# Layer norm scalings moved from ScalarE to VectorE, and two subtractions of the second layer's cut from GpSimd to VectorE

## The chip, the cores and the metric

The kernel runs on one core of one Trainium2 chip. The metric is the device time of one execution in microseconds (us), and lower is better. Five engines of the core work in parallel and meet at semaphores: TensorE (PE, with its weight loads PEld), VectorE (DVE), ScalarE (ACT), GpSimd (POOL) and SyncE (SP), which issues most of the DMAs.

## What is computed

Two layers on an x of 8 batches x 512 tokens x 128 channels, all in f32. Cut to what matters here:

```python
def _layernorm(x, axis=-1, eps=1e-05):
    m = jnp.mean(x, axis=axis, keepdims=True)
    v = jnp.var(x, axis=axis, keepdims=True)
    return (x - m) / jnp.sqrt(v + eps)
...
    x = L0_attn_x
    xn = _layernorm(x, axis=-1)
    x = x + _L0_attn_ref(xn, ...) + _L0_ffn_ref(xn, ...)
    xn = _layernorm(x, axis=-1)
    x = x + _L1_attn_ref(xn, ...) + _L1_ffn_ref(xn, ...)
    return x
```

Layer 0 is an attention over the 16 heads of one token, with a low-rank key and value projection and rotary angles, plus a gated feed-forward block. The attention of layer 1 is a Mamba mixer: it starts with an RMS norm of xn (so that xn is scaled a second time), makes a step dt, an input u and the vectors B and C for each token, and then runs the recurrence `h = exp(dt * A) * h + dt * B * u` over 512 tokens for 256 channels x 16 states, from which `y = sum(h * C)`. The feed-forward block of layer 1 is a mixture of 8 experts, two for each token, with one shared expert.

## The kernel before

**Tiling.** A batch is 512 tokens; a tile of tokens x channels is [128 partitions, TT = 4 groups of tokens, 128 channels], and turned by TensorE it is [128 channels, 512 tokens]. `layer0` handles the 8 batches in a software pipeline, one turn of its loop for a batch; `layer1` then does the recurrence batch by batch. Each engine has its own program, written out in the functions `gpsimd`, `scalar`, `vector` and `tensor`: the order of an engine's instructions is the order of its calls, and it waits in that order. Nothing is reordered when the kernel runs. A semaphore is wrapped in `Count`, so that `x.at(b, n)` is its value after the n-th step of batch b.

**Layer norm in layer 0.** Three engines make it. DVE takes the mean and variance (`statistics`, L767 to L775), POOL the power -0.5 (`root`, L518), DVE the product -mean * rstd (`shift_mean`, L780, tile `below`), and ACT applies it as `rstd * x + below`, one instruction of 128x128 for each of the four groups (`normalize`, L604, tile `xn`). PE then turns xn (`turn_x`, L1066), ACT copies it out of PSUM, and the projections follow (L1071 to L1087). The result of a batch is normalized again for layer 1: DVE's `pre_statistics` (L864 to L880), POOL's `second_root` (L539), DVE's `pre_means` (L884 to L888, tile `below2`), and ACT's `pre_normalize` with four instructions that write xn (L610; the tile `rows` lies in the memory that the profile calls `slots`) and four for the doubly normalized `xnr` (L616). PE turns both (L1184). The last batch is normalized so at the beginning of layer 1, in the calls of `tail`.

**Layer 1.** A batch has GROUPS = 32 steps, k = 0 to 31. In a step PE spreads one group of the input over the partitions (`spread_du`, L2098, into one of two PSUM banks `p_s_du`), DVE multiplies it by B (`inject`, L1980) and runs the recurrence (`scan`, L1988, tile `hs`), and ACT has made the decays three steps ahead (`decay`, L1881). After every second step POOL multiplies the two new tiles of hs by C (`times_c`, L1729), and after every fourth PE sums them (`gather_y`, L2112), standing in its queue ahead of the next `spread_du`. So POOL's pace reaches DVE through PE.

**Preparing the next batch.** In between, step by step, batch b + 1 is prepared while batch b is in the recurrence: softplus on ACT and DVE (L1959, L1964), `steps` on POOL (L1706, L1710, at k = 16 and 18), and the cut of dt * u into three bf16 parts whose sum is the f32 value. That cut is the chain that the change touches, for each of two halves s: ACT rounds the first part (`first_part`, L1856, k = 19 and 23); POOL subtracts it (`second_rest`, L1715, k = 20 and 24, tile `rest`, which shares memory with `conv`); ACT rounds the second part (`second_part`, L1860, k = 21 and 25); POOL subtracts again (`third_part`, L1720, k = 22 and 26). For batch 1 the same four subtractions are done by DVE, during layer 0 (L1969, L1974). The parts then go by DMA into the tile that PE spreads.

**What else stands in these queues.** POOL sends rows to the experts in batches 1 to 3 of layer 1 (L1747) and gathers the experts' sums in batches 4 to 8 (L1763), mostly at even steps; both are indirect DMAs that POOL issues. In batch 8, DVE takes five of the sixteen `times_c` (L1995). DVE also multiplies the experts' gate and up products (`half`, L2013), and ACT computes the gate's silu (L1896) after PE's down product of the unit before (L2171).

## Time and profile before

| | |
|---|---|
| median of 3 runs | 1091.25 us (1085.58 to 1091.52) |
| the profiled execution | 1085.58 us |
| its span in the trace | 1083.8 us, so 1.8 us lie around it |
| DVE busy | 869.2 us, 80% of the span |
| PE busy | 802.5 us, 74% |
| POOL busy | 632.8 us, 58% |
| ACT busy | 566.0 us, 52% |
| DMA engines | about 60% of the span |
| layer 0, until DVE's first scan | 446 us |
| layer 1 | the other 638 us, 74.6 to 78.5 us for a batch after the first |

An engine's busy share is an average over two layers with different limits. The first place to look is therefore the stage: busy time by engine in a stretch, then the waits in that stretch, then single instructions in order of time. "L1729" is line 1729 of the kernel before; an arrow `<-` in a wait names what ended it. Busy times of instructions that overlap at their ends are added up whole.

### The profile page before, as it was taken

How to read it: one execution, taken by the hardware profiler on the slowest of the kernel's cores; microseconds unless marked ns; L12 is line 12 of the kernel's file. 1: busy time of each engine (PE TensorE's matmuls, PEld its weight loads, DVE VectorE, ACT ScalarE, POOL GpSimd, SP SyncE). 2: the span in 40 equal slices, each digit the busy share in tenths (PEclk: the TensorE clock that was granted, in tenths of full speed). 3: DMA queues.
4: the chain of work that ended last, by engine and by line, in shares of the span. 5: the costliest groups of instructions: out<-in, count | busy, mean ns of one | idle time of the engine just before them, and what ended most of it. 6: DMA issues, size and time to landing. Idle time of an engine off the chain costs nothing. (4 is left out here: it accounts for less than half of the span.)

```text
span 1083.8 us, 12247 instructions
## 1 busy us (share of the span) xinstructions
PE 802.5 (74%) x3584; PEld 377.2 (35%) x3584; DVE 869.2 (80%) x1154; ACT 566.0 (52%) x888; POOL 632.8 (58%) x385
## 2 busy tenths in 40 slices
PE   3658778788797867488888789788888788743645
PEld 1112333333333323334544445344445444301211
DVE  2547878879778554689899899998898898995997
ACT  1122334333342353457787787786777776743420
POOL 1021121211221376337979979669989889689995
PEclk9659898898998897769999999899999999955665
DMA  4996568576562048451882873756957848626411
GB/s 131 220 196 164 152 147 224 160 175 195 146 160 83 15 119 219 117 153 40 240 240 80 212 226 97 190 153 159 241 140 180 200 115 192 157 48 137 82 20 35
DMA packets 85023, 161.48 MB, mean 149 GB/s; under 512 B 12603, under 2 KB 54748, under 8 KB 76636
## 3 DMA queue, kind: packets, MB, share of 16 engines
q1 hardware_dynamic: 73692, 152.26, 54.1%
q0 software_dynamic: 11264, 8.43, 4.6%
q8 instruction: 29, 0.48, 0.2%
q14 instruction: 38, 0.31, 0.1%
HBM read 116.26 MB, written 31.80 MB: 137 GB/s over the span
## 5 line engine op out<-in xcount | busy, mean ns | idle before, releaser
L1729 POOL TENSOR_TENSOR hs<-hs,c_rep 128x1024 f32<-128x1024 f32 x123 | 324.5, 2649 | 76.4 <-DVE hs L1988 75.6
L1980 DVE TENSOR_TENSOR p_s_du<-p_s_du,b_rep 128x512 f32<-128x512 f32 x256 | 174.4, 681 | 25.9 <-PE p_s_du L2098 25.5
L2098 PE MATMUL p_s_du<-block_in,spread 96*128 96x512 bf16 x256 | 110.2, 437 | 110.3 <-DVE hs L1988 110.0
L1988 DVE TENSOR_TENSOR_SCAN hs<-slots,p_s_du 128x512 f32<-128x512 f32 x108 | 131.8, 1221 | 10.8
L831 DVE TENSOR_TENSOR value_prod<-p_eb_y_acc,v 128x512 f32<-128x512 f32 x128 | 83.9, 685 | 39.4 <-PE p_eb_y_acc L1133 38.9
L1988 DVE TENSOR_TENSOR_SCAN hs<-steps,p_s_du 128x512 f32<-128x512 f32 x88 | 107.4, 1221 | 9.1 <-DVE p_s_du L1980 0.5
L1763 POOL DMA_INDIRECT y_xr<-moe_sums,position x64 | 103.0, 1610 | 11.6 <-issue 9.5
L522 POOL TENSOR_TENSOR sc<-ex,ex_part 128x1024 f32<-128x1024 f32 x8 | 17.0, 2128 | 157.5 <-ACT ex_part L647 157.5
L2112 PE MATMUL p_eb_y_acc<-hs,gather 128*32 128x512 f32 x512 | 81.1, 711 | 24.1 <-POOL hs L1729 19.4
L2098 PEld LDWEIGHTS p_s_du<-block_in,spread 96*128 96x128 bf16 x256 | 25.7, 101 | 202.7 <-DVE hs L1988 167.6
L807 DVE TENSOR_TENSOR score_prod<-qb,p_k_misc 128x2048 f32<-128x2048 f32 x32 | 72.4, 2283 | 13.0 <-issue 7.0
L1896 ACT ACTIVATE sg<-p_a_gu 128x1024 f32<-128x1024 f32 (+1 forms) x32 | 31.8, 994 | 59.1 <-PE p_acc_o L2171 47.9
L1881 ACT ACTIVATE steps<-steps,a_neg 128x512 f32<-128x512 f32 x88 | 60.1, 718 | 0.1
L539 POOL TENSOR_TENSOR root<-var,half 128x8 f32<-128x8 f32 x8 | 13.2, 1646 | 78.7 <-DVE var L880 78.7
L1988 DVE TENSOR_TENSOR_SCAN hs<-y_xr,p_s_du 128x512 f32<-128x512 f32 x44 | 53.7, 1221 | 4.7 <-DVE p_s_du L1980 0.5
L2070 PE MATMUL p_k_misc<-y_ht,wtap 128*128 128x512 f32 x112 | 56.9, 613 | 0.0
L2171 PEld LDWEIGHTS p_acc_o<-wm,sg 128*128 128x128 f32 x368 | 49.2, 198 | 17.4 <-issue 16.0
L2151 PE MATMUL p_a_gu<-xgt,wm 128*128 128x256 f32 x184 | 48.8, 388 | 3.3 <-ACT sg L1896 3.3
L2171 PE MATMUL p_acc_o<-wm,sg 128*128 128x128 f32 x368 | 51.1, 284 | 0.0
L1133 PE MATMUL p_eb_y_acc<-stack,over_d 96*128 96x512 bf16 x128 | 42.4, 390 | 10.8 <-DVE value_prod L831 9.9
L2140 PE MATMUL p_a_gu<-xgt,wm 128*128 128x256 f32 x184 | 49.2, 391 | 0.6 <-issue 0.4
L1881 ACT ACTIVATE slots<-slots,a_neg 128x512 f32<-128x512 f32 x60 | 40.9, 719 | 13.1 <-DVE hs L1988 13.0
(203 smaller groups left out, 1749.8 us busy)
## 6 DMA issues: line engine op xcount, KB each, us to landing
qb<-rq_rows SPq DMA_DIRECT2D x32, 1024.0 KB, 13.7
...
```

Source lines behind the costliest of these rows:

```text
L807: nc.vector.tensor_tensor(score_prod[:, i % 2], qb[:, i], p_k[:].unsqueeze(1).to_broadcast([128, 4, T]), ALU.mult)\
L831: nc.vector.tensor_tensor(value_prod[:, n % NP], p_eb[:, n % 2], v[:, b % NV], ALU.mult).then_inc(weighed.sem, 1)
L1729: nc.gpsimd.tensor_tensor(hs[:, n:n + 2], hs[:, n:n + 2], c, ALU.mult)\
L1763: nc.gpsimd.indirect_dma_start(xr[:, b - 1, t], None, moe["sums"][grp], bass.IndirectOffsetOnAxis(ap=position[:, grp, kk, TT * i + t:TT * ...
L1881: nc.scalar.activation(decay_of(b, k), steps_of[n % 3][:, bass.ts(j, T)], ACT.Exp, scale=a_neg[:, g:g + 1]).then_inc(da_done.sem, 1)
L1980: nc.vector.tensor_tensor(p_du[:, k % 2], p_du[:, k % 2], b_rep[p][:, order[k][3]], ALU.mult).then_inc(dbu_done.sem, 1)
L1988: nc.vector.tensor_tensor_scan(hs[:, n % NA], decay_of(b, k), p_du[:, k % 2], 0.0, ALU.mult, ALU.add).then_inc(scanned.sem, 1)
L2070: ins = nc.tensor.matmul(bank(b, U0 + n)[:, :], wtap[:, k, bass.ts(n, 128)], ht[:, b % 2, k:k + T], start=(k == 0), stop=(k == CONV - 1))
L2098: nc.tensor.matmul(p_du[:, k % 2], spread[:, i], block_in[:, (2 * b + s) % NB, j], start=True, stop=True).then_inc(du_full.sem, 1)
L2112: ins = nc.tensor.matmul(p_y[32 * j:32 * j + 32], w["gather"][:, i], hs[:, (GROUPS * (b - 1) + k) % NA], start=(i == 0 and h == 0), stop=( ...
L2140: ins = nc.tensor.matmul(p_gu[:, t, bass.ts(f, 256)], wm[:, (2 * j + t) % NR, bass.ts(f, 128)], xgt[:, j % 2, t], start=True, stop=True)
L2171: ins = nc.tensor.matmul(p_o[:, bass.ts(2 * t + i, 128)], sg[:, t, 256 * f + 128 * i:256 * f + 128 * i + 128], wm[:, (2 * j + t) % NR, 2 * ...
```

## The change

Two edits. The scaling of the layer norms becomes one DVE instruction for each group of 128x128, `(x - mean) * rstd` with both as values for each partition, and the products `below` and `below2`, their semaphores and their tiles go. And from batch 2 on the two subtractions of the cut are called in DVE's program at the same steps k, where they had been in POOL's.

```diff
@@ gpsimd of layer 0
         def root(b):
             pool.wait_ge(ln_var.sem, ln_var.at(b))
-            pool.wait_ge(ln_done.sem, ln_done.at(b - 1))
@@ residual
-            pool.wait_ge(pre_done.sem, pre_done.at(b, 1))
+            pool.wait_ge(pre_done.sem, pre_done.at(b, 2))
@@ scalar of layer 0
-        def normalize(b):
-            act.wait_ge(ln_shift.sem, ln_shift.at(b))
-            act.wait_ge(xt_full.sem, xt_full.at(b - 1))
-            for t in range(TT):
-                ins = nc.scalar.activation(xn[:, t], x[:, -b % NX, t], ACT.Identity, bias=below[:, t:t + 1], scale=rstd[:, t:t + 1])
-            ins.then_inc(ln_done.sem, 1)
...
@@ vector of layer 0
-        def shift_mean(b):
+        def normalize(b):
             dve.wait_ge(ln_rstd.sem, ln_rstd.at(b))
-            dve.wait_ge(ln_done.sem, ln_done.at(b - 1))
-            nc.vector.scalar_tensor_tensor(below[:], mv[:, :, 0], -1.0, rstd[:], ALU.mult, ALU.mult).then_inc(ln_shift.sem, 1)
+            dve.wait_ge(xt_full.sem, xt_full.at(b - 1))
+            for t in range(TT):
+                ins = nc.vector.tensor_scalar(xn[:, t], x[:, -b % NX, t], mv[:, t, 0:1], rstd[:, t:t + 1], ALU.subtract, ALU.mult)
+            ins.then_inc(ln_done.sem, 1)
...
-        def pre_means(b):
+        def pre_normalize(b):
             dve.wait_ge(pre_root.sem, pre_root.at(b))
-            nc.vector.tensor_tensor(rr[:], root2[:, 0], root2[:, 1], ALU.mult).then_inc(pre_shift.sem, 1)
-            dve.wait_ge(pre_done.sem, pre_done.at(b - 1))
-            nc.vector.scalar_tensor_tensor(below2[:, 0], mv2[:, :, 0], -1.0, root2[:, 0], ALU.mult, ALU.mult).then_inc(pre_shift.sem, 1)
-            dve.wait_ge(pre_shift.sem, pre_shift.at(b, 1))
-            nc.vector.scalar_tensor_tensor(below2[:, 1], mv2[:, :, 0], -1.0, rr[:], ALU.mult, ALU.mult).then_inc(pre_shift.sem, 1)
+            nc.vector.tensor_tensor(rr[:], root2[:, 0], root2[:, 1], ALU.mult).then_inc(pre_done.sem, 1)
+            for t in range(TT):
+                ins = nc.vector.tensor_scalar(rows[:, TT * (b - 1) + t, 0:D], x1[:, b % 2, t], mv2[:, t, 0:1], root2[:, 0, t:t + 1],
+                                              ALU.subtract, ALU.mult)
+            ins.then_inc(pre_done.sem, 1)
+            dve.wait_ge(pre_done.sem, pre_done.at(b, 1))
+            dve.wait_ge(pre_full.sem, pre_full.at(b - 1, 2))
+            for t in range(TT):
+                ins = nc.vector.tensor_scalar(xnr[:, t], x1[:, b % 2, t], mv2[:, t, 0:1], rr[:, t:t + 1], ALU.subtract, ALU.mult)
+            ins.then_inc(pre_done.sem, 1)
@@ gpsimd of layer 1, batch
-                if nxt and k in (20, 24):
-                    second_rest(b + 1, (k - 20) // 4)
-                if nxt and k in (22, 26):
-                    third_part(b + 1, (k - 22) // 4)
@@ vector of layer 1, batch
                 if k == 15:
                     softplus_end(b + 1)
+                if k in (20, 24):
+                    second_rest(b + 1, (k - 20) // 4)
+                if k in (22, 26):
+                    third_part(b + 1, (k - 22) // 4)
```

The lines of the changed kernel are numbered anew: `inject` is L1943 there, `scan` L1951, `half` L1976, the two subtractions L1932 and L1937, `times_c` of POOL L1696.

On DVE in layer 0, from the reciprocal of the softmax's denominators (tile `rden`) to the rotation of the queries (tile `turn`), before:

```order
L850 RECIPROCAL rden<-p_a_gu 128x512
L780 SCALAR_TENSOR_TENSOR below<-mv,rstd 128x4
L857 TENSOR_TENSOR x<-p_acc_o,x 128x512
L807 TENSOR_TENSOR score_prod<-qb,p_k_misc 128x2048
L864 BN_STATS stats<-x 128x6 x4
...
L807 TENSOR_TENSOR score_prod<-qb,p_k_misc 128x2048
L884 TENSOR_TENSOR rr<-root 128x4
L886 SCALAR_TENSOR_TENSOR below<-mv,root 128x4
L888 SCALAR_TENSOR_TENSOR below<-mv,rr 128x4
L785 SCALAR_TENSOR_TENSOR turn<-p_a_gu,bq,rope 128x512
```

and now:

```order
L822 RECIPROCAL rden<-p_a_gu 128x512
L751 TENSOR_SCALAR xn<-x,mv,rstd 128x128 x4
L829 TENSOR_TENSOR x<-p_acc_o,x 128x512
L779 TENSOR_TENSOR score_prod<-qb,p_k_misc 128x2048
L836 BN_STATS stats<-x 128x6 x4
...
L779 TENSOR_TENSOR score_prod<-qb,p_k_misc 128x2048
L856 TENSOR_TENSOR rr<-root 128x4
L858 TENSOR_SCALAR slots<-x,mv,root 128x128 x4
L864 TENSOR_SCALAR xnr<-x,mv,rr 128x128 x4
L757 SCALAR_TENSOR_TENSOR turn<-p_a_gu,bq,rope 128x512
```

Three instructions of 128x4 have become twelve of 128x128, and ACT no longer stands between `rstd` and PE.

On DVE in batch 1 of layer 1, from step k = 20 to k = 24, before:

```order
L1988 SCALAR_TENSOR_TENSOR hs<-slots,p_s_du 128x512
L2001 SCALAR_TENSOR_TENSOR yt<-u,vecs,p_eb_y_acc 128x512
L1980 TENSOR_TENSOR p_s_du<-p_s_du,b_rep 128x512
L1988 SCALAR_TENSOR_TENSOR hs<-slots,p_s_du 128x512
L1980 TENSOR_TENSOR p_s_du<-p_s_du,b_rep 128x512
L1988 SCALAR_TENSOR_TENSOR hs<-slots,p_s_du 128x512
L2013 SCALAR_TENSOR_TENSOR sg<-p_a_gu,sg 128x1024
L1980 TENSOR_TENSOR p_s_du<-p_s_du,b_rep 128x512
```

and now:

```order
L1951 SCALAR_TENSOR_TENSOR hs<-slots,p_s_du 128x512
L1964 SCALAR_TENSOR_TENSOR yt<-u,vecs,p_eb_y_acc 128x512
L1932 TENSOR_TENSOR conv<-dtu,y_part 128x512
L1943 TENSOR_TENSOR p_s_du<-p_s_du,b_rep 128x512
L1951 SCALAR_TENSOR_TENSOR hs<-slots,p_s_du 128x512
L1943 TENSOR_TENSOR p_s_du<-p_s_du,b_rep 128x512
L1951 SCALAR_TENSOR_TENSOR hs<-slots,p_s_du 128x512
L1976 SCALAR_TENSOR_TENSOR sg<-p_a_gu,sg 128x1024
L1937 TENSOR_TENSOR y_part<-conv,y_part 128x512
L1943 TENSOR_TENSOR p_s_du<-p_s_du,b_rep 128x512
```

A subtraction stands behind step 20 and another behind step 22, ahead of the next step's `inject`; two more follow behind steps 24 and 26.

On POOL in batch 3, from the second pair of `steps` (L1706, L1710) to the third `times_c` behind it, before:

```order
L1706 TENSOR_TENSOR dtu<-dtu 128x512
L1710 TENSOR_TENSOR dtu<-dtu,u 128x512
L1729 TENSOR_TENSOR hs<-hs,c_rep 128x1024
L1715 TENSOR_TENSOR conv<-dtu,y_part 128x512
L1736 TENSOR_TENSOR yt<-yt,sz 128x512
L1729 TENSOR_TENSOR hs<-hs,c_rep 128x1024
L1720 TENSOR_TENSOR y_part<-conv,y_part 128x512
L1729 TENSOR_TENSOR hs<-hs,c_rep 128x1024
```

and now:

```order
L1683 TENSOR_TENSOR dtu<-dtu 128x512
L1687 TENSOR_TENSOR dtu<-dtu,u 128x512
L1696 TENSOR_TENSOR hs<-hs,c_rep 128x1024
L1703 TENSOR_TENSOR yt<-yt,sz 128x512
L1696 TENSOR_TENSOR hs<-hs,c_rep 128x1024 x8
```

Of POOL's queue only the `times_c`, the gating of y (`yt`) and the indirect DMAs of other batches are left there.

## Rows read from the trace of the kernel before

**Rows 1.** The page, busy time, share of the span and instructions.

```profile
PE 802.5 (74%) x3584; PEld 377.2 (35%) x3584; DVE 869.2 (80%) x1154; ACT 566.0 (52%) x888; POOL 632.8 (58%) x385
```

**Rows 2.** Batches 3, 5, 7: us, busy PE PEld DVE ACT POOL, PEclk, DMA, GB/s.

```profile
613.00:687.00 74.00, 62.04 (x317) 35.13 (x310) 68.24 (x74) 58.85 (x92) 59.57 (x35) 1.00 0.66 174
763.00:841.00 78.00, 62.93 (x308) 35.81 (x300) 69.98 (x74) 59.24 (x92) 72.70 (x41) 0.98 0.74 186
919.00:996.00 77.00, 41.88 (x160) 15.06 (x156) 64.91 (x72) 43.65 (x66) 62.43 (x35) 0.68 0.50 113
```

**Rows 3.** Waits of DVE in layer 1, 446 to 1073 us.

```profile
DVE p_s_du L1980 <- PE p_s_du L2098: 25.5, 15, 5.8
DVE sg L2013 <- PE p_a_gu L2151: 7.4, 6, 2.0
```

**Rows 4.** Waits from 948 to 1005 us (end of batch 7): DVE, PE, POOL.

```profile
DVE p_s_du L1980 <- PE p_s_du L2098: 12.3, 3, 5.8
PE p_eb_y_acc L2112 <- POOL hs L1729: 13.9, 3, 6.2
POOL hs L1729 <- DVE hs L1988: 2.2, 2, 1.6
```

**Rows 5.** Groups by line: line, engine, out<-in | busy, mean ns | idle before.

```profile
L1729 POOL TENSOR_TENSOR hs<-hs,c_rep 128x1024 f32<-128x1024 f32 x123 | 324.5, 2649 | 76.4 <-DVE hs L1988 75.6
L1715 POOL TENSOR_TENSOR conv<-dtu,y_part 128x512 f32<-128x512 f32 x14 | 21.1, 1507 | 0.0
L1969 DVE TENSOR_TENSOR conv<-dtu,y_part 128x512 f32<-128x512 f32 x2 | 1.4, 688 | 9.4 <-ACT y_part L1856 9.4
```

**Rows 6.** Timeline of layer 0, a run of equal instructions on DVE: start, us.

```profile
227.16 2.48 DVE L831 TENSOR_TENSOR value_prod<-p_eb_y_acc,v 128x512 f32<-128x512 f32 x4
```

**Rows 7.** Timeline of batch 8: DVE's `times_c` beside POOL's work.

```profile
1044.36 2.95 POOL L1729 TENSOR_TENSOR hs<-hs,c_rep 128x1024 f32<-128x1024 f32 x1
1044.42 3.98 DVE L1995 TENSOR_TENSOR hs<-hs,c_rep 128x1024 f32<-128x1024 f32 x1
...
1059.55 1.56 POOL L1763 DMA_INDIRECT y_xr<-moe_sums,position  x1 [0.16 <-issue]
1060.57 1.23 DVE L1995 TENSOR_TENSOR hs<-hs,c_rep 128x1024 f32<-128x1024 f32 x1
```

**Rows 8.** Timeline of batch 2 around step k = 20.

```profile
587.29 1.02 ACT L1896 ACTIVATE sg<-p_a_gu 128x1024 f32<-128x1024 f32 x1 [3.08 <-PE p_acc_o L2171]
587.47 0.72 DVE L2001 SCALAR_TENSOR_TENSOR yt<-u,vecs,p_eb_y_acc 128x512 f32<-128x512 f32 x1
588.22 0.62 ACT L1856 ACTIVATE y_part<-dtu 128x512 bf16<-128x512 f32 x1
588.96 2.37 POOL L1729 TENSOR_TENSOR hs<-hs,c_rep 128x1024 f32<-128x1024 f32 x1
```

**Rows 9.** Waits of DVE around step 29, in batch 4, then in batch 2.

```profile
DVE sg L2013 <- PE p_a_gu L2151: 2.0, 1, 2.0
DVE p_s_du L1980 <- PE p_s_du L2098: 1.0, 1, 1.0
...
DVE sg L2013 <- PE p_a_gu L2151: 0.5, 1, 0.5
```

**Rows 10.** Timeline of layer 0, one turn of the loop.

```profile
248.21 1.65 ACT L604 ACTIVATE xn<-x,below,rstd 128x128 f32<-128x128 f32 x4 [10.64 <-DVE below L780]
249.91 0.66 PE L1066 MATMUL p_a_gu<-ident,xn 128*128 128x128 f32 x4 [2.79 <-ACT xn L604]
250.88 0.87 DVE L864 BATCH_NORM_STATS2 stats<-x 128x6 f32<-128x128 f32 x4
257.76 0.76 DVE L787 SCALAR_TENSOR_TENSOR p_a_gu<-p_a_gu,bq,rope 128x512 f32<-128x512 f32 x1 [0.69 <-PE p_a_gu L1077]
```

**Rows 11.** Timeline of the first steps of layer 1: PE, then DVE.

```profile
455.49 1.11 PE L1184 MATMUL p_acc_o<-ident,slots 128*128 128x128 f32 x4 [1.66 <-ACT slots L610]
462.08 0.70 DVE L1980 TENSOR_TENSOR p_s_du<-p_s_du,b_rep 128x512 f32<-128x512 f32 x1 [2.44 <-PE p_s_du L2098]
465.92 0.70 DVE L1980 TENSOR_TENSOR p_s_du<-p_s_du,b_rep 128x512 f32<-128x512 f32 x1 [1.82 <-PE p_s_du L2098]
```

47 lines of the change are left out of this document (9 added, 38 removed).

## Prediction

> **What bounds the kernel now.** I read the page first, then busy time by batch, then the waits of each layer, and last single instructions in order of time. The page has DVE as the busiest engine, with 80% of the span [rows 1]; but that is a mean over two layers. In layer 1, 446 us to the end, DVE is busy for 68.2 of 74 us in batch 3 and 70.0 of 78 in batch 5 [rows 2]. What it waits for there is short: 25.5 us for the next `p_s_du` of PE and 7.4 us for the experts' up product, of 627 us [rows 3]. So nearly everything put on DVE in layer 1 is put on the path.
>
> POOL is the second actor. In batch 5 it is busy for 72.7 of 78 us, in batch 3 only for 59.6 of 74 [rows 2]. It reaches DVE by way of PE, which stands at `gather_y` until POOL has multiplied, with DVE's next input queued behind. Where that happens is shown by the waits by stretch: 12.3 of the 25.5 us lie in the last third of batch 7 and the first steps of batch 8, where PE waits 13.9 us for POOL and POOL only 2.2 us for a scan [rows 4]. There POOL is the bound. In batches 4 to 6 POOL's lag costs DVE less: around step 29 of batch 4 it waits 2.0 and 1.0 us, in batch 2, with a shorter lag, 0.5 and nothing [rows 9]; 2.5 us for a batch. In batches 1 to 3 the DVE waits that are left follow PE's own queue.
>
> **Layer 1, the subtractions: DVE's own time.** Seven preparations (batches 2 to 8) with four subtractions each make 28 instructions more on DVE. One of this form takes 688 ns [rows 5]. In a row of equal ones the next starts before the last has ended: four take 2.48 us [rows 6], so the pitch is (2.48 - 0.69) / 3 = 0.60 us. That is 28 x 0.60 = 16.8 us, on the path.
>
> **What they wait for.** `second_rest` stands in DVE's queue right behind step 20, and the `inject` of step 21, with all of PE behind it, is queued behind it. It needs ACT's first part, and ACT makes that only after the silu at 587.29, which PE's down product has held up for 3.08 us. In batch 2 DVE is free about 588.1 (the 0.72 us from 587.47, less the overlap), and the first part is ready at 588.84 [rows 8]: 0.75 us of waiting. ACT's second silu of that kind, at step 25, does the same to the last subtraction at step 26. Both come before batches 2 to 7; in batch 7 there are no experts' products left and the wait isn't there. 6 x 1.5 = 9 us. Bounds: nothing, if PE and ACT run ahead once DVE is slower, and 14 us.
>
> **The port.** `conv<-dtu,y_part` has both inputs in SBUF; `inject` and `scan` have one in PSUM. Before shows what such an instruction of DVE does beside POOL: `times_c` on DVE takes 1.23 us when POOL is at an indirect DMA, but 3.98 us when POOL's `times_c` began 0.06 us ahead of it, and it ends 1.09 us after POOL's end (1048.40 against 1047.31) [rows 7]. So it stands still until POOL's instruction is over. The Trainium skill ("SBUF — State Buffer", Who interferes with whom) says that a DVE instruction with two SBUF inputs and a GpSimd instruction that reads SBUF exclude each other for a whole instruction, the first to start going first. By that rule each of the 28 instructions is exposed, and the trace agrees with it.
>
> The price of one meeting lies between 0 and 3.98 - 1.23 = 2.75 us [rows 7]. POOL's `times_c` takes 2.37 us early [rows 8] and 2.95 us late [rows 7]; sixteen of them are 38 us of batch 3's 74 and 47 us of batch 5's 78, 51 to 60% of the time, and more where POOL is late; with 65% in these steps a chance meeting costs half of one: 0.65 x 2.37 / 2 = 0.8 us early and 0.65 x 2.95 / 2 = 1.0 late, 3.2 and 4.0 us for four. Walking through batch 2 gives less, as the waits overlap: the first subtraction is ready at 588.9, in a tie with POOL's 588.96 [rows 8] (0 or 2.4 us); whichever wins, the second or third meets the next `times_c` for the rest of it. I get 2.6 us for the four in batches 1, 2 and 4 to 6, 0.7 in batch 3, where POOL is not late.
>
> **What comes back.** POOL loses four instructions of 1.5 us (1507 ns [rows 5]; about 1.2 us early and 1.75 late), 6 to 7 us for a batch. In batches 1 to 3 DVE didn't wait for that, so nothing comes back. In batches 4 to 6 the 2.5 us of a batch do [rows 9]. At the end of batch 7, where POOL is the bound, its 7 us are saved, and DVE's new work lies in waits that it had anyway; but POOL in its turn stands still while DVE's subtractions run, 4 x 0.6 = 2.4 us. I take -5.5 us; the bounds are 0 and all 12.3 us of [rows 4].
>
> Sum for layer 1, for each preparation, own time + ACT + port - returned: batches 1 and 2: 2.4 + 1.5 + 2.6 = 6.5 each; batch 3: 2.4 + 1.5 + 0.7 = 4.6; batches 4 to 6: 6.5 - 2.5 = 4.0 each; batch 7: -5.5. That is 13.0 + 4.6 + 12.0 - 5.5 = +24 us.
>
> **Layer 0.** DVE gets 12 instructions of 128x128 in a turn, and loses two small ones of 0.1 us and one that ran beside others. The trace has no such instruction in a row; the nearest is bn_stats of the same size, four in 0.87 us [rows 10], 0.2 us each. With two values for each partition I take the same 0.2: 2.4 us more, less 0.3, +2.1 in a turn; bounds 0.13 and 0.3 us each, 1.3 to 3.3 us in a turn. 
>
> What comes back in a turn: ACT's four take 1.65 us and PE waits 2.79 us for them [rows 10]. DVE has xn done about 1 us earlier; PE and the whole chain to the queries start that much sooner, and DVE's wait of 0.69 us for them [rows 10] goes; I count on another 0.6 us of its later waits for PE in the turn. That leaves about +0.8 us in each of six turns with a second normalization, nothing in the first two, where loads are waited for: +4 us (-4 to +12). At the start of layer 1, ACT's four for batch 8 hold PE up for 1.66 us, and DVE soon waits 2.44 and 1.82 us for PE [rows 11]. DVE pays 1.3 us more there and these waits shrink: -1.5 us (-3 to +1.3).
>
> **Sum.** 24 + 4 - 1.5 = +26.5 us on the profiled execution's 1085.6 (span 1083.8 and 1.8 around it): 1112.1 us. The median shown is 5.7 us above that execution. The changed kernel's median will lie likewise above, and I add half: 1115 us.
>
> **Rivals.**
> *The port costs nothing* and ACT is early. Then layer 1 is 16.8 - 7.5 - 7 = about +2, the whole +5: 1091 to 1097 us. For it: small DVE instructions beside POOL mostly don't stretch, and at steps 22 to 26 a slower DVE gives POOL time to finish. Against it: the 3.98 us, and that POOL is at work 75 to 93% of these batches [rows 2]. The port decides as soon as half of the 28 meet a `times_c`.
>
> *POOL is the bound from batch 4 on*, not only in batch 7. Then each of four batches gives back 7.0 - 2.4 = 4.6 us and DVE's additions are covered there: -18; batches 1 to 3 cost 3 x 2.4 = +7; and in layer 0 the shorter chain wins about 0.9 us in each of eight turns, -7. 1085.6 - 18 = 1068 us, faster. It decides if POOL has no idle time between a scan's end and its `times_c` over a whole batch. For it: 72.7 of 78 us in batch 5. Against it: 59.6 of 74 in batch 3, and DVE's few waits in batches 4 to 6.
>
> *Every subtraction meets a fresh `times_c`*, since POOL starts at the end of odd steps and the subtractions stand behind even ones, so that phases lock. 28 x (0.60 + 2.1) = 76 us, less 20 returned, +4: 1145 us.
>
> *The slower DVE starves PE* until its granted clock falls in batches 1 to 6, as it has in batch 7 (0.68 against 1.00 in batch 3 [rows 2]). PE's work would then show in DVE's waits: some us in each batch, and the time is 1125 to 1140 us.
>
> **Chances.** A measurement of this kernel tells about 1% from no change. My forecast's case, +12 to +40 us: 0.6. Port free: 0.2. POOL the bound: 0.1. The two dearer ones: 0.1 together. The low end of the range is that of the port-free case less a little for layer 0, 1088; the high end, 1137, leaves out the phase lock. Faster by over 1%: 0.09. Within 1%: 0.22, the port-free case and the low edge of mine. Slower by over 1% (above 1102): 0.69.
>
> **What would show it.** DVE's two subtraction lines at a mean well above 0.69 us, 1.2 to 1.6, with single ones near 3; POOL's instructions stretched by up to 0.6 us beside them; waits of DVE for ACT's parts near 0.75 us, twelve times; PE's waits for POOL in batches 4 to 8 mostly gone; batches 1 to 3 longer by 5 to 6 us, batch 7 shorter; a turn of layer 0 longer by under 1 us. If the subtractions average 0.7 us, the port step is wrong; if batches 4 to 6 are shorter than before, POOL was their bound; if layer 0 changes by more than 10 us, my pitch for the small ones is.

## The result, and the profile after

| | before | changed |
|---|---|---|
| median, us | 1091.38 (1085.58 to 1091.58) | 1140.57 (1135.68 to 1142.24) |
| profiled execution, span, us | 1083.8 | 1138.9 |
| first scan of layer 1 at, us | 445.85 | 470.75 |
| first scan to the end of the last, us | 627.4 | 657.6 |

The changed kernel is slower: ratio 1.0443, 95% interval 1.039 to 1.0498. The prediction said slower, at 1115 us; the result is 26 us above that and 3.6 us above the range. Of the profile's 55 us, 25 lie in layer 0, where 4 were forecast, and 30 in layer 1, where 24 were.

The page, as in [rows 1]:

```profile
PE 834.1 (73%) x3584; PEld 391.6 (34%) x3584; DVE 940.7 (83%) x1254; ACT 528.1 (46%) x792; POOL 605.2 (53%) x357
```

DVE is busy for 71.5 us more, with 100 more instructions. The 28 subtractions of layer 1 at 0.69 us would be 19 of these and the change in layer 0 some 22 (8 turns of 2.75, below); 30 us are not accounted for by such work. Batches 3, 5 and 7 of the changed kernel, as in [rows 2]:

```profile
652.00:729.00 77.00, 61.99 (x315) 35.32 (x311) 72.35 (x79) 59.08 (x92) 52.75 (x29) 1.00 0.60 158
810.00:894.00 84.00, 65.86 (x322) 37.27 (x321) 77.52 (x80) 59.29 (x92) 66.21 (x35) 0.96 0.66 169
976.00:1053.00 77.00, 42.44 (x153) 14.17 (x155) 72.67 (x76) 43.75 (x66) 61.14 (x32) 0.66 0.52 114
```

The granted clock in layer 1 is nearly what it was (1.00, 0.96, 0.66 against 1.00, 0.98, 0.68), so the starved-PE rival isn't at work there. POOL is busy for 7, 6 and 1 us less, and DVE for 4, 8 and 8 us more.

The waits of DVE in layer 1, which answer to [rows 3], and from 1020 us the waits for POOL, which answer to [rows 4]:

```profile
DVE conv L1932 <- ACT y_part L1819: 4.5, 6, 1.5
DVE p_s_du L1943 <- PE p_s_du L2065: 4.0, 4, 1.8
...
DVE y_part L1937 <- ACT y_part L1823: 1.9, 1, 1.9
...
PE p_eb_y_acc L2079 <- POOL hs L1696: 4.2, 4, 1.4
```

DVE's 25.5 us of waiting for the next product shrank to 4.0, and PE's wait for POOL at the end of batch 7 from 13.9 to 4.2: the relief of POOL is real. The two subtraction lines of DVE swallowed it. Groups by line, mean in ns:

```profile
L1932 DVE TENSOR_TENSOR conv<-dtu,y_part 128x512 f32<-128x512 f32 x16 | 33.2, 2075 | 11.7 <-ACT y_part L1819 11.7
L1937 DVE TENSOR_TENSOR y_part<-conv,y_part 128x512 bf16<-128x512 f32 x16 | 19.6, 1226 | 1.9 <-ACT y_part L1823 1.9
```

The timeline of batch 2 behind step 20, POOL and DVE together, and then that of batch 5:

```profile
620.44 4.45 DVE L1932 TENSOR_TENSOR conv<-dtu,y_part 128x512 f32<-128x512 f32 x1 [1.46 <-ACT y_part L1819]
620.75 2.36 POOL L1696 TENSOR_TENSOR hs<-hs,c_rep 128x1024 f32<-128x1024 f32 x1
623.06 1.27 POOL L1703 TENSOR_TENSOR yt<-yt,sz 128x512 f32<-128x512 f32 x1
...
860.95 5.37 DVE L1932 TENSOR_TENSOR conv<-dtu,y_part 128x512 f32<-128x512 f32 x1 [0.68 <-ACT y_part L1819]
861.59 2.96 POOL L1696 TENSOR_TENSOR hs<-hs,c_rep 128x1024 f32<-128x1024 f32 x1
863.90 1.86 POOL L1703 TENSOR_TENSOR yt<-yt,sz 128x512 f32<-128x512 f32 x1
```

Read the ends. POOL's second instruction ends at 624.33, DVE's subtraction at 624.89; at 865.76 and 866.32 in batch 5. DVE waited through two instructions of POOL in a row and ended 0.56 us behind the second, though it had begun 0.31 and 0.64 us before the first. 21 of the 28 subtractions meet POOL in this way, and all 21 end 0.55 to 0.56 us after POOL does. The 28 take 50.1 us; alone they would take 28 x 0.69 = 19.3. So the port costs DVE 30.8 us, in a layer that grew by 30.2. POOL's `times_c` are not stretched in return: they take 2.51 us in the mean, before 2.65.

The trace of before had such meetings already. DVE's first softplus instruction (L1959, two operands in SBUF, 1.22 us alone), in batch 2:

```profile
570.01 3.80 DVE L1959 SCALAR_TENSOR_TENSOR dtu<-conv,dtu 128x1024 f32<-128x1024 f32 x1
570.33 2.39 POOL L1729 TENSOR_TENSOR hs<-hs,c_rep 128x1024 f32<-128x1024 f32 x1
```

It began 0.32 us ahead of POOL's product and ended 1.09 us behind it. The other six of layer 1 met POOL too and took 1.32 to 3.09 us.

In layer 0 I take a turn from one `RECIPROCAL rden` of DVE to the next. Turn 3 before, then turns 3 and 4 after (busy PE, PEld, DVE, ACT, POOL, then PEclk):

```profile
156.52:200.61 44.09, 36.10 (x178) 14.78 (x178) 35.92 (x61) 16.54 (x28) 9.29 (x6) 0.92 0.68 180
```

```profile
161.31:207.41 46.10, 38.12 (x178) 15.53 (x178) 38.74 (x71) 11.71 (x16) 9.28 (x6) 0.89 0.67 172
207.41:257.86 50.45, 40.12 (x178) 16.68 (x178) 39.97 (x72) 11.71 (x16) 9.30 (x6) 0.86 0.61 157
```

DVE is busy 2.8 us longer in a turn (turn 4 has 1.2 us of setup for layer 1 in it, before as well). In turn 3 the rest of the turn, in which DVE isn't busy, is 7.4 us, in turn 4 10.5; before it was 8.2. The same turn 4 in stretches of 4 us:

```profile
220.00:224.00 4.00, 1.02 (x9) 0.71 (x6) 4.00 (x11) 1.09 (x2) 0.00 (x0) 1.00 0.31 68
224.00:228.00 4.00, 3.73 (x8) 1.18 (x7) 3.97 (x4) 0.00 (x0) 0.00 (x0) 0.65 0.17 66
228.00:232.00 4.00, 4.00 (x18) 2.21 (x18) 3.97 (x6) 2.08 (x3) 0.00 (x0) 0.50 0.77 197
232.00:236.00 4.00, 4.00 (x11) 0.61 (x12) 0.57 (x1) 0.30 (x2) 0.00 (x0) 0.50 1.01 217
236.00:240.00 4.00, 4.00 (x20) 2.18 (x18) 3.54 (x6) 0.87 (x2) 0.00 (x0) 0.65 1.04 229
```

PE had 1.02 us of work in 220 to 224 us; then its granted clock fell to 0.50, that is to 1.2 of 2.4 GHz, just as it had work without a gap, and from 232 to 236 us it was DVE that had next to nothing to do (0.57 of 4 us). What PE stood still for is in the timeline:

```profile
219.65 1.10 DVE L858 TENSOR_SCALAR slots<-x,mv,root 128x128 f32<-128x128 f32 x4
220.67 1.10 DVE L864 TENSOR_SCALAR xnr<-x,mv,rr 128x128 f32<-128x128 f32 x4
...
223.71 1.12 PE L1058 MATMUL p_a_gu<-lat,wup 33*128 33x512 f32 x2 [2.25 <-DVE turn L757]
...
236.29 1.29 DVE L803 TENSOR_TENSOR value_prod<-p_eb_y_acc,v 128x512 f32<-128x512 f32 x2 [3.72 <-PE p_eb_y_acc L1110]
```

The rotation of the queries (L757) had to stand behind the eight scalings and the setup. Four scalings start 1.02 us before the next four, 0.255 us each.

So three questions: is the port the whole of layer 1's loss; how much of layer 0's is DVE's own work and how much the clock; and do the two halves add up?

### The profile page after: what moved, and what is told of

It reads as the page before. It is cut to its first block and busy times, and to the rows that moved or that the text cites. A ratio compares the mean times of both kernels' runs of the same rounds, so it can differ in the third digit from the quotient of the medians.

```text
span 1138.9 us, 12206 instructions
## 1 busy us (share of the span) xinstructions
PE 834.1 (73%) x3584; PEld 391.6 (34%) x3584; DVE 940.7 (83%) x1254; ACT 528.1 (46%) x792; POOL 605.2 (53%) x357
## 5 line engine op out<-in xcount | busy, mean ns | idle before, releaser
L1696 POOL TENSOR_TENSOR hs<-hs,c_rep 128x1024 f32<-128x1024 f32 x123 | 309.3, 2514 | 131.3 <-DVE hs L1951 130.9
L2065 PE MATMUL p_s_du<-block_in,spread 96*128 96x512 bf16 x256 | 112.5, 442 | 165.4 <-DVE hs L1951 165.0
L1943 DVE TENSOR_TENSOR p_s_du<-p_s_du,b_rep 128x512 f32<-128x512 f32 x256 | 174.0, 680 | 4.2 <-PE p_s_du L2065 4.0
L1951 DVE TENSOR_TENSOR_SCAN hs<-slots,p_s_du 128x512 f32<-128x512 f32 x108 | 131.8, 1220 | 11.1 <-DVE p_s_du L1943 0.5
L1951 DVE TENSOR_TENSOR_SCAN hs<-steps,p_s_du 128x512 f32<-128x512 f32 x88 | 107.4, 1220 | 9.1 <-issue 0.4
L1730 POOL DMA_INDIRECT y_xr<-moe_sums,position x64 | 106.3, 1661 | 11.5 <-issue 8.2
L2037 PE MATMUL p_k_misc<-y_ht,wtap 128*128 128x512 f32 x112 | 60.3, 645 | 0.0
L534 POOL TENSOR_TENSOR root<-var,half 128x8 f32<-128x8 f32 x8 | 13.2, 1646 | 83.9 <-DVE var L852 83.9
L1951 DVE TENSOR_TENSOR_SCAN hs<-y_xr,p_s_du 128x512 f32<-128x512 f32 x44 | 53.7, 1220 | 4.7 <-DVE p_s_du L1943 0.5
L1074 PE MATMUL p_s_du<-score_prod,sum_d 128*32 128x512 f32 x256 | 48.0, 832 | 13.0 <-DVE score_prod L779 13.0
L2118 PE MATMUL p_a_gu<-xgt,wm 128*128 128x256 f32 x184 | 51.4, 404 | 1.9 <-ACT sg L1859 1.9
L1110 PE MATMUL p_eb_y_acc<-stack,over_d 96*128 96x512 bf16 x128 | 45.1, 413 | 9.2 <-DVE value_prod L803 7.3
L2107 PE MATMUL p_a_gu<-xgt,wm 128*128 128x256 f32 x184 | 50.5, 398 | 0.0
```

The costliest lines, as they stand in the source:

```text
L1696: nc.gpsimd.tensor_tensor(hs[:, n:n + 2], hs[:, n:n + 2], c, ALU.mult)\
L1730: nc.gpsimd.indirect_dma_start(xr[:, b - 1, t], None, moe["sums"][grp], bass.IndirectOffsetOnAxis(ap=position[:, grp, kk, TT * i + t:TT * ...
L1943: nc.vector.tensor_tensor(p_du[:, k % 2], p_du[:, k % 2], b_rep[p][:, order[k][3]], ALU.mult).then_inc(dbu_done.sem, 1)
L1951: nc.vector.tensor_tensor_scan(hs[:, n % NA], decay_of(b, k), p_du[:, k % 2], 0.0, ALU.mult, ALU.add).then_inc(scanned.sem, 1)
L2037: ins = nc.tensor.matmul(bank(b, U0 + n)[:, :], wtap[:, k, bass.ts(n, 128)], ht[:, b % 2, k:k + T], start=(k == 0), stop=(k == CONV - 1))
L2065: nc.tensor.matmul(p_du[:, k % 2], spread[:, i], block_in[:, (2 * b + s) % NB, j], start=True, stop=True).then_inc(du_full.sem, 1)
```

## The experiments

The kernel before was run beside each group: its median was 1095.5 us in the first, 1094.6 in the second and third, 1094.1 in the fourth.

### Each half alone

`e1_layer0_only` has the changed kernel's layer 0 and the subtractions on POOL; `e2_layer1_only` has the reverse.

```diff
 # e1, vector: batch()
-                if k in (20, 24):
-                    second_rest(b + 1, (k - 20) // 4)
-                if k in (22, 26):
-                    third_part(b + 1, (k - 22) // 4)
 # e1, gpsimd: batch()
+                if nxt and k in (20, 24):
+                    second_rest(b + 1, (k - 20) // 4)
+                if nxt and k in (22, 26):
+                    third_part(b + 1, (k - 22) // 4)
```

Expected of e1: 

> The layer norm edit alone: the scalings on DVE, the subtractions back on POOL. The two traces put DVE's first scan at 446 us before and 471 us after, so theory A (the two edits add up, and layer 0 alone has lost about 25 us, six times what I forecast) gives 1091 + 25 = 1116 us, with the first scan at 470 to 472. Theory B (layer 0 costs the 4 us of my sum and the rest of the 25 was brought about by something else, so that the edits don't add) gives 1095 us.

Expected of e2: 

> The subtractions alone on DVE, the scalings back on ACT. Theory A: layer 1 is 30 us longer as in the changed kernel, batch by batch +7, +8, +2, +6, +5, +4, 0, and the first scan stands at 446 us: 1121 us. My forecast for layer 1 by itself was +24, 1115 us. Theory B: the subtractions cost only DVE's own 17 us less what POOL's relief gives back: under 1105 us.

Measured: e1 1108.69 us, ratio 1.0113 (1.0064 to 1.0162); e2 1121.36 us, ratio 1.0226 (1.0167 to 1.0285). Both halves lose. e1 lies between its two forecasts: layer 0's part costs 13 us in the medians, not the 25 by which the two profiles differ. e2 is where theory A had it. The sum of the two, 3.4%, is under the first measurement of both together (4.4%) and near the second (3.9%, below). In e2 the 28 subtractions take 50.6 us, one by one nearly the durations of the changed kernel, with layer 0 untouched.

### Layer 0 in doses

`e3_norm_only` moves only the first normalization to DVE (4 scalings in a turn), `e4_pre_only` only the second (8). In both the subtractions stay on POOL.

```diff
 # e3, vector: main()
-            shift_mean(1)
+            normalize(1)
 # e4, vector: main()
-                    pre_means(b - 2)
+                    pre_normalize(b - 2)
```

Expected of e3: 

> Of the layer norm edit only the first normalization (four scalings of a batch, tile xn) on DVE; the second stays on ACT with its small products. It shortens the chain to PE by about 0.6 us and costs DVE 4 x 0.25 us less 0.1. Theory C (DVE's time costs what it is): between -2 and +6 us over eight batches, 1089 to 1097. Theory D (what costs is TensorE's clock, which falls after PE has been kept waiting, so that anything that feeds PE sooner is a gain): -5 to 0 us.

Expected of e4: 

> Only the second normalization (eight scalings of a batch) on DVE, the first on ACT as before. Theory D: this is the part that keeps PE waiting 2.3 us for the rotated queries and shifts the stretch at granted clock 0.5 into PE's fullest 12 us; nearly all of the 25 us is here: 1110 to 1116 us. Theory C (DVE's time alone): 8 x 0.25 = 2.0 us in a turn, 6 turns and the tail: +10 to +14 us, 1101 to 1105.

Measured: e3 1100.46 us, ratio 1.0022 (0.9978 to 1.0066); e4 1102.5 us, ratio 1.0078 (1.0042 to 1.0114). The first normalization alone costs nothing that can be told, though its median lies above both forecasts. The second alone costs what theory C gave it, far under theory D's; its 0.8% can't be told from the 1.1% of all twelve scalings.

### The scalings elsewhere, fewer of them, and once more

`e5_scalings_later` is the changed kernel with the four scalings into `xnr` behind `rope_q`; `k1_one_scaling` makes one instruction of each four, with the mean and factor of the first group for all four, so it leaves out the normalization of the other three; `a2_after_again` is the changed kernel itself.

```diff
 # e5, vector: main()
                 if b < B:
                     rope_q(b + 1)
+                if pre and new:
+                    pre_normalize_late(b - 2)
 # k1, in the three places
-            for t in range(TT):
-                ins = nc.vector.tensor_scalar(xn[:, t], x[:, -b % NX, t], mv[:, t, 0:1], rstd[:, t:t + 1], ...)
+            ins = nc.vector.tensor_scalar(xn[:], x[:, -b % NX], mv[:, 0, 0:1], rstd[:, 0:1], ...)
```

Expected of e5: 

> The changed kernel with one thing moved: the four scalings into xnr stand behind the three instructions that rotate the next batch's queries, not ahead of them (for the last but one batch they stay where they were). VectorE has the same work. If layer 0's loss is VectorE's own added time, nothing changes: 1139 to 1143 us, ratio 1.044, a first scan near 470 us. If it comes from TensorE waiting for the rotated queries and then working through the rest of the turn at a granted clock of 0.50, that wait (2.25 us) shrinks by about the 1.1 us of the four scalings, fewer turns have such a stretch, and the first scan comes at 455 to 462 us, the kernel at 1124 to 1132, ratio 1.030 to 1.036.

Expected of a2: 

> The changed kernel once more, for a second look at its layer 0. If the length of a turn goes by where TensorE's granted clock falls to 0.50 in it, the turns differ from the first profile's (48.8, 46.1, 50.5, 48.4, 46.9 us) or agree with them exactly as their low stretches do; the time is 1135 to 1143 us, ratio 1.040 to 1.049. If VectorE's own work set the turns, they would be as long in the run with layer 0's part alone (45.3, 45.3, 49.6, 45.2, 44.1), which they were not.

Expected of k1: 

> The changed kernel with each group of four 128x128 scalings of layer 0 as one instruction of 128x512, which takes the mean and factor of the first tile for all four, so the normalization of the other three tiles is left out. A group of four took 1.10 us; one of 128x512 should take 0.3 to 0.7 us. If VectorE's own added work is layer 0's loss, 1.2 to 2.4 us go from each turn: first scan 452 to 459 us instead of 466 to 471, ratio 1.026 to 1.032. If the loss is the granted clock or a wait, the turns keep their lengths: ratio 1.037 to 1.045.

Measured: e5 1136.87 us, ratio 1.0417 (1.0349 to 1.0485); a2 1137.7 us, ratio 1.039 (1.0317 to 1.0464); k1 1125.83 us, ratio 1.0277 (1.0216 to 1.0339). e5 moved four of the eight scalings ahead of the rotation out of PE's way; its time lies between its two forecasts, nearer to that of no change, and can't be told from a2's; its first scan comes at 465.4 us. a2's turns 2 to 6 (46.2, 48.2, 50.5, 45.2, 44.0 us) are not those of the first profile of the same kernel (48.8, 46.1, 50.5, 48.4, 46.8). Cutting their time did: in k1 one scaling of 128x512 takes 0.54 us where four of 128x128 took 1.10, and the kernel is 12 us faster than a2.

### TensorE's gaps filled

Two useless products on PE ahead of the turn of x in six turns, in the kernel before (`f1_before_filled`); the same and two more ahead of `project_k` in the changed kernel (`f2_after_filled`).

```diff
 # tensor: turn_x(b), for b > 2
+                for _ in range(2):
+                    nc.tensor.matmul(p_a0[:], wq[:, 0], xt[:, (b - 2) % NT], start=True, stop=True)
 # f2 also, main(): ahead of project_k(b + 1)
+                    for _ in range(2):
+                        nc.tensor.matmul(p_s[:, 1], wq[:, 0], xt[:, b % NT], start=True, stop=True)
```

Expected of f1: 

> The kernel before with two useless products (a 128x128 weight by 128x512, f32, 1.05 us each, written where the turn of x follows and overwrites them) on TensorE in six turns of layer 0, in the gap of 2.8 us in which it waits for the normalized x. All other engines have the same work. Clock theory: it is the thin work at the start of a turn after which the granted clock falls to 0.50 for some 6 to 8 us; with the gap filled it falls in fewer turns, a turn goes from 44.0 us toward the 41.1 us of the one turn seen without a low stretch, and the first scan comes at 432 to 443 us instead of 446 to 452; kernel 1077 to 1088, ratio 0.985 to 0.995. Rival, that the low stretch is covered by VectorE's work and costs nothing, or that two products change nothing about it: 1.000 within 0.4%, first scan 446 to 452.

Expected of f2: 

> The changed kernel with the same two products in the gap ahead of the turn of x, and two more in the 2.25 us in which TensorE waits for the rotated queries, behind the first transposes of the older batch. VectorE has exactly the work of the changed kernel, TensorE has more. Clock theory: the stretches at 0.50 in the middle of the turns go or shrink, turns 2 to 6 go from a mean of 47.1 us to 43 to 45, the first scan from 466 to 471 to 445 to 455, the kernel from 1138 to 1115 to 1125, ratio 1.022 to 1.030. Rival, VectorE's added time alone: the turns stay at 46 to 50 us, ratio 1.039 to 1.046.

Measured: f1 1091.03 us, ratio 0.9972 (0.9936 to 1.0007); f2 1133.14 us, ratio 1.0323 (1.0248 to 1.0398). Neither can be told from its kernel without the products; f2 lies between its two forecasts. Turn 2 of f1, and turn 2 of before for comparison:

```profile
113.36:155.93 42.57, 35.54 (x182) 14.91 (x182) 35.83 (x62) 16.60 (x29) 9.30 (x6) 1.00 0.67 169
```

```profile
112.40:156.52 44.12, 36.01 (x178) 14.80 (x178) 35.92 (x61) 16.72 (x29) 9.29 (x6) 0.92 0.63 163
```

There the clock stayed at 1.00 for the whole turn, and the turn was 1.55 us shorter at the same work of DVE: that is what the low stretch early in a turn costs the kernel before. But in turns 3 to 6 of f1 the stretch was there as ever. In f2 the turns took 46 to 48 us. The filling didn't remove the low stretches where it mattered, so the clock's share rests on comparing turns, not on an intervention.

### What a turn consists of

Mean of turns 2 to 6 in the profiles, from windows like those above:

| kernels (turns) | turn, us | DVE busy | the rest (least to most) |
|---|---|---|---|
| layer 0 as before: before, e2, e6, e7, g1, h1 (30) | 44.07 | 35.90 | 8.16 (6.6 to 9.6) |
| e3, 4 scalings (5) | 44.31 | 36.75 | 7.55 (6.7 to 10.1) |
| e4, 8 scalings (5) | 44.65 | 37.67 | 6.98 (6.6 to 7.9) |
| all 12: after, a2, e1, m1 (20) | 47.07 | 38.65 | 8.42 (6.6 to 10.5) |
| k1, 12 as 3 (5) | 45.32 | 37.04 | 8.28 (7.3 to 9.8) |

DVE's busy time follows the dose: +0.85, +1.8, +2.75 us, a net 0.23 us for each scaling. The rest, in which DVE isn't busy, is never under 6.6 to 7.3 us in any row. Two things move it.

The first is the low stretch early in the turn. With ACT's scalings the granted clock falls to 0.50 for some 7 us, in three turns for 10, beginning 5 to 7 us into the turn, and the rest is 8.1 to 8.4 us in most turns; in turn 6 of e6 and turn 2 of f1 and g2, without a low stretch, it is 6.6 to 6.7. With DVE's scalings an early stretch hardly lengthens the turn. Turn 2 of e1, with DVE's, and turn 2 of e2, with ACT's, both have one of 10.2 us that begins about 5 us into the turn:

```profile
115.32:160.61 45.29, 37.84 (x178) 14.98 (x178) 38.57 (x70) 11.89 (x17) 9.29 (x6) 0.89 0.64 159
114.67:160.28 45.61, 37.50 (x178) 15.12 (x178) 36.07 (x61) 16.73 (x29) 9.29 (x6) 0.89 0.61 156
```

The rest is 6.7 us in the first and 9.5 in the second, though DVE has 2.5 us more to do in the first.

The second is a low stretch in the middle. Of the 20 turns with all twelve scalings, ten have a rest of 6.6 to 7.5 us (mean 6.9) and ten one of 9.5 to 10.5 (mean 9.9). The second ten are those with the clock at 0.50 for over 10 us, beginning 17 to 20 us into the turn, as in turn 4 above; in the first ten such a stretch is missing or takes 3.4 us. Of the 30 turns with ACT's scalings none has one. Two turns of e1 show both levels, with the same instructions but for the 1.2 us of setup in turn 4:

```profile
160.61:205.94 45.33, 35.61 (x178) 14.64 (x178) 38.57 (x70) 11.71 (x16) 9.30 (x6) 0.96 0.68 175
205.94:255.58 49.64, 41.31 (x178) 16.75 (x178) 39.97 (x72) 11.71 (x16) 9.29 (x6) 0.83 0.63 159
```

So the rest is the same in the mean (8.16 and 8.42 us), but it is put together differently: 1.2 us come back in half of the turns, and 1.7 are added in the other half. In the mean over all turns the 3.0 us are DVE's own work, 2.75, and 0.26 of rest, and k1 agrees: 1.6 us less work in a turn, 1.7 us less turn.

### Layer 1: other places for the subtractions

`e6_odd_steps` is e2 with the subtractions between `inject` and `scan` of odd steps. `h1_late_odd_steps` has them two steps later, with ACT's and SyncE's part moved along. `g1_three_on_vector` leaves the first of the four on POOL, and `g2_three_and_filled` adds the products of f1.

```diff
 # e6, vector: batch()
                     inject(b, p, k)
+                    if nxt and k in (21, 25):        # h1: (23, 27)
+                        second_rest(b + 1, (k - 21) // 4)
+                    if nxt and k in (23, 27):        # h1: (25, 29)
+                        third_part(b + 1, (k - 23) // 4)
                     scan(b, k)
```

Expected of e6: 

> The kernel before with the subtractions of layer 1 on VectorE, but placed between the product and the scan of the odd steps 21, 23, 25 and 27 instead of behind the even steps 20, 22, 24 and 26. Port theory: at 23, 25 and 27 the multiplication of the pair before is over on GpSimd, so each takes 0.68 us instead of 1.05 to 1.18; at step 21 the pair and the gate still run and it may still take up to 4 us. Against the 1121 us of the run with them behind the even steps this gives 1108 to 1116, ratio to the kernel before 1.010 to 1.018; with step 21 free as well 1100, ratio 1.005. Rival, that any instruction here costs its place in the chain of scans and its wait for ScalarE whatever runs on GpSimd: 1119 to 1123, ratio 1.022 to 1.026.

Expected of g1: 

> The kernel before with three of the four subtractions of a preparation in layer 1 on VectorE, at the odd steps 23, 25 and 27, and the first, which at step 21 collided with GpSimd for 3.2 to 5.4 us in five of seven batches, left on GpSimd at step 20. Nothing is left out. Port theory: in batches 1 to 6 each of the three takes 0.68 us, and the kernel is at the 1086 us of the run with a PSUM operand or a few us over it: 1084 to 1092, ratio 0.990 to 0.998. Rival, that what made the PSUM run fast was less of something else than the port: 1096 to 1106, as the odd-step run (1.011).

Expected of g2: 

> Both together: three subtractions on VectorE at the odd steps, and the two useless products in the gap ahead of the turn of x. If the two effects are independent their ratios multiply: with 0.994 and 0.990 that is 0.984, 1077 us. If layer 1 gives back what layer 0 gains, it is no faster than the better of the two.

Expected of h1: 

> The kernel before with layer 1's subtractions on VectorE between the product and the scan of the odd steps 23, 25, 27 and 29 (ScalarE's second roundings at 24 and 28 instead of 21 and 25, SyncE's copies of the parts one to four steps later). Nothing is left out. Where the odd-step run had them, steps 23, 25 and 27 took 0.68 us nearly always and step 21 up to 5.4. Port theory: all four take 0.68 to 0.9 us, the kernel comes to within 5 us of the run with an operand in PSUM: 1085 to 1091, ratio 0.991 to 0.997. Rival, that the first subtraction meets GpSimd wherever it stands, since the delay it causes makes GpSimd late: 1100 to 1106, ratio 1.006 to 1.011.

Measured: e6 1104.05 us, ratio 1.0111 (1.0048 to 1.0174), 17 us under e2; g1 1102.84 us, ratio 1.0089 (1.0051 to 1.0128); g2 1098.49 us, ratio 1.0031 (0.999 to 1.0073); h1 1115.06 us, ratio 1.0196 (1.0139 to 1.0253). The port theory's forecasts for g1, g2 and h1 (1084 to 1092, 1077, 1085 to 1091) all failed, since they took the new places for free. Every place that was picked from the trace of another placement met POOL again. Batch 5 of e6, POOL and DVE:

```profile
827.17 5.36 DVE L1955 TENSOR_TENSOR conv<-dtu,y_part 128x512 f32<-128x512 f32 x1
827.81 2.96 POOL L1719 TENSOR_TENSOR hs<-hs,c_rep 128x1024 f32<-128x1024 f32 x1
830.12 1.86 POOL L1726 TENSOR_TENSOR yt<-yt,sz 128x512 f32<-128x512 f32 x1
```

The end again lies 0.55 us behind POOL's (832.53 against 831.98). In e6 11 of 28 meet POOL, in h1 13. In e6 the long meetings stand at step 21 in batches 1, 5 and 6, but at step 25 in batch 2 and at step 23 in batch 4; in batches 1 to 6 of h1 (2.97 to 4.79 us) at step 23 in batches 1 and 4 and at step 27 in 2, 5 and 6. When I wrote the expectations of g1 and h1 I had the durations of e6 in one row and took all five for step 21. They are not tied to a step: wherever the first meeting comes, it lets POOL catch up and shifts what follows. g1's 21 instructions meet POOL 14 times. h1 is dearer than its meetings alone say (table below): DVE waits 20.0 us for PE's product there (15 times), where it waits 9.0 in e6 (4 times). Which of h1's moves brings these waits wasn't looked into. g2 is g1 with 4 us less, which its interval can't tell from it.

### Layer 1: without the port

`e7_one_operand_from_psum` is e6 with an instruction of the same size in place of the subtraction, one operand in PSUM; `m1_after_from_psum` is the changed kernel with the same, also at e6's odd steps.

```diff
 # e7, second_rest(b, s); third_part likewise
-            nc.vector.tensor_tensor(rest[:, s], dtu[:, 1, s], part[:, s, 0], ALU.subtract)
+            nc.vector.scalar_tensor_tensor(rest[:, s], p_du[:, 1], 0.0, dtu[:, 1, s], ALU.mult, ALU.add)
```

Expected of e7: 

> As the run with the subtractions at the odd steps, but each is replaced by an instruction of the same size with one operand in PSUM (0 times the step's product plus the other operand), so the subtraction itself is left out and the parts are not the reference's. Port theory: all four take 0.70 to 0.75 us, at step 21 too, and none waits for GpSimd; the kernel is 0 to 15 us under the odd-step run, by whatever its step 21 lost to GpSimd. Rival: the duration at step 21 stays at 3 us and more because it is a wait for something else, and the two runs agree within 0.3%.

Expected of m1: 

> The changed kernel with layer 1's subtractions replaced as in the PSUM run (0 times the step's product plus the other operand, between product and scan of steps 21, 23, 25, 27; the subtraction is left out). Then only layer 0's part is left of the loss: with 18 us of it on the PSUM run's 1086 that is 1104, ratio 1.009; the sum forecast for layer 0 (4 us) would give 1090, ratio 0.996. If layer 1's loss in the changed kernel were more than the port, it stays above 1.015.

Measured: e7 1086.21 us, ratio 0.9928 (0.9891 to 0.9965); m1 1100.44 us, ratio 1.0052 (1.0021 to 1.0082). The groups of e7:

```profile
L1955 DVE SCALAR_TENSOR_TENSOR conv<-p_s_du,dtu 128x512 f32<-128x512 f32 x16 | 11.0, 690 | 10.8 <-ACT y_part L1842 9.5 <-DVE p_s_du L1966 0.4
L1960 DVE SCALAR_TENSOR_TENSOR y_part<-p_s_du,conv 128x512 bf16<-128x512 f32 x16 | 11.0, 690 | 0.5
```

23 of the 28 overlap a product of POOL, and none is held up: each takes 0.69 us. That the instruction is another one doesn't explain it: the softplus of before is a `SCALAR_TENSOR_TENSOR` too, with both operands in SBUF, and was held up. One of them, in batch 4 (DVE, POOL):

```profile
739.61 0.69 DVE L1955 SCALAR_TENSOR_TENSOR conv<-p_s_du,dtu 128x512 f32<-128x512 f32 x1
740.27 2.97 POOL L1719 TENSOR_TENSOR hs<-hs,c_rep 128x1024 f32<-128x1024 f32 x1
```

It starts 0.66 us ahead of POOL's product; the subtraction that started 0.64 us ahead in the changed kernel's batch 5 took 5.37 us. Side by side, with the 28 (g1: 21) durations summed and 0.69 us for each taken off:

| | port, us | layer 1, us | median, us |
|---|---|---|---|
| before | none | 627.4 | 1091 to 1095 |
| e7 | 0.0 | 623.1 | 1086.2 |
| g1 | 22.9 | 638.0 | 1102.8 |
| e6 | 25.2 | 641.1 | 1104.1 |
| h1 | 20.7 | 646.8 | 1115.1 |
| e2 | 31.3 | 662.9 | 1121.4 |
| after | 30.8 | 657.6 | 1140.6 |

With no port, DVE takes all 28 instructions and layer 1 is 4 us shorter than before, since POOL's relief pays for more than their 19 us: DVE's waits for PE's product fall from 25.5 to 15.6 us, those for the experts' products from 12.0 to 5.1. e7 is the fastest kernel of the study, but it leaves the subtraction out; of the versions that compute the parts none beats the kernel before. One that kept one of the two operands in PSUM might; it wasn't tried, since all eight banks hold something in layer 1. Layer 0's price, by m1 against e7 (the only difference), is 14.2 us, and 13.2 by e1 against before.

## Why the prediction was right in direction and short by half

**DVE bounds layer 1, so what is put on it is on the path.** Right for the port's 31 us, wrong for plain work: in e7, where the 28 stand at odd steps, their 19.3 us cost nothing. I let only 7.5 us of batches 4 to 6 and the relief of batch 7 come back; in the changed kernel DVE's waits for PE went from 25.5 to 4.0 us in all. The rival with the port free put layer 1 at +2; it was -4.

**Own time, 0.60 us each.** Right: 0.69 us long in e7, overlapping its neighbours as expected.

**Waits for ACT, 6 x 1.5 = 9 us.** Half right. Six waits for the first part, 4.5 us in all, 0.75 in the mean as worked out (0.3 to 1.5), but of the six at step 26 only one came (1.9 us): the subtraction before had already held DVE long enough.

**The port.** This step failed in size. The mechanism, a whole instruction of POOL waited out, was as taken from [rows 7], and by the same rule of the Trainium skill ("SBUF — State Buffer", Who interferes with whom). But I priced a meeting as half of one `times_c`, 2.6 us for a preparation and 13.7 in batches 1 to 6; the runs show 25.2 there, and 5.6 in batch 7, for which I had put on nothing. Three things were left out. A second instruction of POOL right behind the first is waited out too (4.01 to 5.39 us, once in each of five batches). A subtraction isn't safe by starting first, not even 0.64 us ahead, which the softplus line of before (570.01) would have told. And step 20's subtraction was bound to meet, as its input comes from ACT just when POOL's product begins: [rows 8] shows the tie (588.84 and 588.96), and I gave it half a chance. The Trainium skill's rule has the first to start go first; by it POOL would have waited for the subtraction of 620.44, and the trace has POOL's product at its usual 2.36 us and DVE at 4.45. These are starts as the profile records them, and POOL's are rough in it; when either asked for the port isn't seen. I also gave POOL "75 to 93%" of these batches, where [rows 2] has 80 to 93.

**Batch 7.** -5.5 us was forecast, -0.1 measured (77.0 to 76.9), and -2.0 in batch 8. PE's waits for POOL went down by 9.7 us, as foreseen; but the four subtractions there met POOL every time and took 2.37, 2.00, 1.50 and 2.47 us. POOL didn't stand still for them, as I had it.

**Batches 1 to 6.** Forecast +6.5 (twice), +4.6, +4.0 (three times); measured +7.0, +7.7, +2.2, +5.8, +4.9, +4.4 us. The parts cancel: the port was nearly twice as dear, and more came back.

**Layer 0.** The second step that failed, in the balance of a turn: +0.8 us a turn and +4 in all were forecast; measured are +3.0 us a turn and +14.2 us between m1 and e7. The profiles show more than the medians: the first scan comes at 446 to 452 us in before, e2, e6, e7, g1 and h1 and at 461 to 471 in after, a2, e1 and m1, 18.5 us apart in the mean. Turns 2 to 6 make 15.0 of these, the time before the first turn 2.1, turn 1 -1.1, and the stretch behind turn 7 2.6. Before and after themselves are 24.9 apart; they lie at the two ends by chance.

Own work is 2.75 us a turn where I had 2.1, as a scaling's pitch is 0.255 us and not bn_stats' 0.2; that stood within the bounds. The 1.3 us of returned waits were right for half of the turns: in the ten without a long low stretch in the middle the rest is 1.2 us under that of before. In the other ten it is 1.7 over, with the clock at 0.50 for over 10 us, and so nothing came back in the mean. I had the starved PE as a rival, but in layer 1, where nothing of the kind came; it stands in layer 0. That DVE's scalings bring these stretches on is likely, since none of the 30 turns with ACT's scalings has one and PE waits 2.25 us behind the scalings, but it is not shown: e4, with the eight scalings ahead of the rotation, has none of that length, e3, without these, has one, e5 took four of them out of the way and kept three, and f2 filled the wait and kept two. What sets one off in one turn and not in the next is open.

**The sum.** The parts don't add up to the first measurement. Layer 1 alone (e2) costs 25.9 us and layer 0 alone (e1) 13.2, 39 together; the changed kernel was 49.2 us over the kernel before at first and 43.1 when run again. Of the 22.7 us between my +26.5 and the 49.2, layer 0 makes 9 by e1, layer 1 with its start 3 by e2, and 10 are what both together cost over the two halves, of which the second measurement shows only 4. No run puts these down to a step.

**The Trainium skill's two elements in a cycle** for f32 `tensor_scalar` ("VectorE: DVE Perf Modes", Mode 2x_2P) agree with the slope. In k1 one scaling of 128x512 starts 0.46 us after the one before it and lasts 0.54; of 128x128 it is 0.255 and 0.33. So 384 elements more cost 0.20 us, 0.52 ns each, while a `tensor_tensor` of DVE (128x512 in 0.69 us, 128x2048 in 2.28) pays 1.04 ns, twice that. The gain was lost on a part that doesn't depend on the size, 0.255 - 128 x 0.00052 = 0.19 us by these figures, which four scalings of 128x128 pay four times. That is what k1 saves: 9 x 0.19 = 1.7 us a turn, 1.6 measured.

The scalings meet the port as well, three times in the changed kernel: in turn 7 (372.09), behind it (428.11) and at the start of layer 1 (479.79). There one of 128x128 takes 1.20 to 1.28 us instead of 0.33 and ends 0.08 us behind POOL's instruction; the four together:

```profile
371.84 1.97 DVE L864 TENSOR_SCALAR xnr<-x,mv,rr 128x128 f32<-128x128 f32 x4
372.00 1.21 POOL L539 TENSOR_TENSOR xr<-x,slots 128x512 f32<-128x512 f32 x1 [1.66 <-DVE slots L858]
```

The sum for layer 0 had no such term; these are 2.7 us.

**The start of layer 1.** -1.5 us forecast; batch 1 of m1 is 1.1 us longer than that of e7 (91.3 and 90.2), and that of e1 0.2 longer than that of before. Nothing came back there.
